# First scatter's ranking: running counts in two PSUM banks used in turn, each count product issued into both

## What is computed

```
edge_index = jnp.stack([src, dst])
x = _layernorm(x + _L0_gnn_ref(x, edge_index, edge_weight, ...))     # three hops: segment_sum(edge_weight * z[col], row)
x = _layernorm(x + _L1_gnn_ref(x, node_type_8, src, dst, edge_type_8, ...))   # typed attention
x = _layernorm(x + _L2_gnn_ref(x, edge_index, ...))                  # attention with leaky relu
x = _layernorm(x + _L3_gnn_ref(x, edge_index, ...))                  # attention, softmax by source
```

## Time and profile before

| | us |
|---|---|
| median of three runs | 10584.68 |
| lowest and highest run | 10577.77, 10587.44 |
| profiled execution, its own time | 10581.93 |
| its span in the profile | 10580.2 |
| TensorE busy | 7483.1 (71%) |
| VectorE busy | 6768.2 (64%) |
| GpSimd busy | 7062.8 (67%) |
| ScalarE busy | 2110.4 (20%) |

### The profile page before, as it was taken

How to read it: one execution, slowest core, us unless ns; L and a number is a source line. 1 busy time by engine, 2 the same in 40 slices (tenths; PEclk the granted TensorE clock), 3 DMA queues, 4 the chain that set the end, 5 groups by cost and what they waited for, 6 DMA issues and landing times. The chain is left out here.

```text
span 10580.2 us, 161564 instructions
## 1 busy us (share of the span) xinstructions
PE 7483.1 (71%) x38345; PEld 5959.2 (56%) x38346; DVE 6768.2 (64%) x21194; ACT 2110.4 (20%) x5705; POOL 7062.8 (67%) x7404
## 2 busy tenths in 40 slices
PE   6999755549998899739105666557774588857776
PEld 4666544436776677624004565456664588846665
DVE  7555566657776777637106777678886455547776
ACT  0333200001111111112002222223332222222222
POOL 1777577767777777767776777057772577737774
PEclk9999955555555555569557888789996655556665
DMA  0000122232223222235104333122222322244443
GB/s 18 2 2 2 24 53 53 52 56 52 53 53 49 62 54 54 52 70 164 50 12 103 104 103 104 28 57 53 51 52 29 83 54 53 54 81 108 108 108 81
DMA packets 434008, 634.20 MB, mean 60 GB/s; under 512 B 163990, under 2 KB 302826, under 8 KB 433034
## 3 DMA queue, kind: packets, MB, share of 16 engines
q0 software_dynamic: 263168, 497.83, 20.3%
q1 hardware_dynamic: 170378, 131.15, 4.3%
HBM read 536.19 MB, written 92.30 MB: 59 GB/s over the span
## 5 line engine op out<-in xcount | busy, mean ns | idle before, releaser
L702 POOL DMA_INDIRECT hop_rows<-hops,k_src_other x1664 | 1571.0, 944 | 553.6 <-issue 497.8
L743 PE MATMUL hop_sums<-hop_rows,hop_weighted 128*128 128x128 f32 x4992 | 1291.8, 440 | 720.6 <-DMA hop_rows<-in_x,k_src_other 449.0
L743 PEld LDWEIGHTS hop_sums<-hop_rows,hop_weighted 128*128 128x128 f32 x4992 | 1109.9, 327 | 874.3 <-DVE hop_odd L788 539.0
L1009 POOL DMA_INDIRECT l_pass_rows<-left_table,k_dst_other x832 | 803.5, 966 | 565.7 <-POOLq L2319 292.0
L1009 POOL DMA_INDIRECT l_pass_rows<-key_table,k_src_other x832 | 787.5, 946 | 509.0 <-POOLq L1616 254.7
L1441 POOL DMA_INDIRECT l_weigh_rows<-row_table,l_weigh_ring x832 | 788.7, 948 | 386.0 <-issue 210.3
L1009 POOL DMA_INDIRECT l_pass_rows<-related,k_dst_typed x832 | 810.4, 974 | 298.1 <-issue 227.0
L702 POOL DMA_INDIRECT hop_rows<-in_x,k_src_other x832 | 785.5, 944 | 303.7 <-issue 253.2
L514 POOL DMA_INDIRECT src_sorted<-src_scatter_records,src_scatter_places x784 | 751.0, 958 | 304.2 <-issue 280.6
L885 POOL DMA_INDIRECT dst_sorted<-rec,dst_places x784 | 762.1, 972 | 277.3 <-issue 238.7
L775 DVE TENSOR_SCALAR hop_weighted<-k_numbers,k_src_place,src_weight 128x128 f32<-128x128 f32 x2496 | 849.9, 402 | 56.3 <-PE hop_sums L743 32.9
(11 more groups left out here) (402 smaller groups left out, 17383.1 us busy)
## 6 DMA issues: line engine op xcount, KB each, us to landing
related<-l_tables_rows SPq DMA_DIRECT2D x50, 1024.0 KB, 4.5
hop_rows<-hops,k_src_other POOLq DMA_INDIRECT x1664, 2.5
hop_rows<-in_x,k_src_other POOLq DMA_INDIRECT x832
l_pass_rows<-related,k_dst_typed POOLq DMA_INDIRECT x832, 2.8
l_pass_rows<-left_table,k_dst_other POOLq DMA_INDIRECT x832, 2.5
l_pass_rows<-key_table,k_src_other POOLq DMA_INDIRECT x832, 2.5
l_weigh_rows<-row_table,l_weigh_ring POOLq DMA_INDIRECT x832
src_sorted<-src_scatter_records,src_scatter_places POOLq DMA_INDIRECT x784
```

The costliest lines, as they stand in the source:

```text
L702: nc.gpsimd.indirect_dma_start(rows[:, s, g, :], None, table_in, bass.IndirectOffsetOnAxis(ap=o.other[:, c:c + 1], axis=0),).then_inc(got[ ...
L743: last = nc.tensor.matmul(sums[:, b, g, :], weighted[:, s % SLOTS, g, :], rows[:, s, g, :], start=True, stop=True)
L1009: nc.gpsimd.indirect_dma_start(rows[:, s, g, :], None, table, bass.IndirectOffsetOnAxis(ap=index[:, c:c + 1], axis=0),).then_inc(got[s], 16)
```

## The change

The table is kept in two PSUM banks. Each one gets every count product, so each product is issued twice, with one column between the two: in column c TensorE issues the product of column c-1 and that of column c into bank (c+1) mod 2, which then holds the table that column c+1 needs. ScalarE copies from bank c mod 2. The wait before the two products asks for one copy less than before (`next_copied` starts at 1), and a new wait ahead of the lookup asks for the copy of column c. The table's start is put into both banks. VectorE clears the one-hots that stand for the column before the first, and waits on line 480 for one lookup more, since the slot's last column is now also read in the next group's first one.

```diff
--- before.py
+++ after.py
@@ -378,7 +378,7 @@
         earlier = sb("earlier", [P, 2, G])
         places = sb("places", [P, SLOTS, G], I32)
         records = sb("records", [P, SLOTS, G, 4])
-        next_ps = ps("next_ps", [HIS, 512])
+        next_ps = ps("next_ps", [HIS, 2, 512])
         turned = ps("turned", [HIS, 2, G, P], BF16)
         nexts = ps("nexts", [P, 2, G, P])
         keyrow = ps("keyrow", [P, 2, G, P])
@@ -418,7 +418,7 @@
 
                         act.wait_ge(next_ready, n * G + g + 1)
                         act.wait_ge(looked, n * G + g + 2 * G - 1)
-                        nc.scalar.copy(next_sb[:, g % 2, :], next_ps[:, 0:P]).then_inc(next_copied, 1)
+                        nc.scalar.copy(next_sb[:, g % 2, :], next_ps[:, g % 2, 0:P]).then_inc(next_copied, 1)
 
             turn_onehots(0, 0)
             in_rounds(act, groups // SLOTS, a_round)
@@ -431,7 +431,10 @@
                 last.then_inc(turned_ok, 1)
 
             pe.sem_inc(looked, 2 * G)
-            nc.tensor.matmul(next_ps[:, 0:P], k.ident[0:HIS, 0:HIS], first_place[:], start=True, stop=False,
+            pe.sem_inc(next_copied, 1)
+            nc.tensor.matmul(next_ps[:, 1, 0:P], k.ident[0:HIS, 0:HIS], first_place[:], start=True, stop=False,
+                             skip_group_check=True)
+            nc.tensor.matmul(next_ps[:, 0, 0:P], k.ident[0:HIS, 0:HIS], first_place[:], start=True, stop=False,
                              skip_group_check=True).then_inc(next_ready, 1)
             pe.wait_ge(onehots, 1)
             turn_onehots(0)
@@ -445,8 +448,13 @@
                     for g in range(G):
 
                         pe.wait_ge(next_copied, n * G + g + 1)
-                        nc.tensor.matmul(next_ps[:, 0:P], oh_hi[:, s, g, :], oh_lo[:, s, g, :], start=False,
+                        s0, g0 = (s, g - 1) if g > 0 else ((s + SLOTS - 1) % SLOTS, G - 1)
+                        nc.tensor.matmul(next_ps[:, 1 - g % 2, 0:P], oh_hi[:, s0, g0, :], oh_lo[:, s0, g0, :], start=False,
+                                         stop=False, skip_group_check=True)
+                        nc.tensor.matmul(next_ps[:, 1 - g % 2, 0:P], oh_hi[:, s, g, :], oh_lo[:, s, g, :], start=False,
                                          stop=False, skip_group_check=True).then_inc(next_ready, 1)
+
+                        pe.wait_ge(next_copied, n * G + g + 2)
                         nc.tensor.matmul(nexts[:, b, g, :], oh_hi_t[:, b, g, :], next_sb[:, g % 2, :], start=True,
                                          stop=True).then_inc(looked, 1)
                         if g == 0:
@@ -467,6 +475,8 @@
                 mark(nc, oh_lo[:, s, :, :], k.numbers, keys[:, 1, here]).then_inc(onehots, 1)
 
             dve.sem_inc(ranked, 2)
+            nc.vector.memset(oh_hi[:, SLOTS - 1, G - 1, :], 0.0)
+            nc.vector.memset(oh_lo[:, SLOTS - 1, G - 1, :], 0.0)
             hot(0, 0)
             hot(1, 1)
 
@@ -477,7 +487,7 @@
 
                     dve.wait_ge(ranked, n + 1)
 
-                    dve.wait_ge(looked, n * G + G)
+                    dve.wait_ge(looked, n * G + G + 1)
                     hot(n + 2, (s + 2) % SLOTS)
 
                     dve.wait_ge(rows, n + 1)
```

## The result

The changed kernel takes 10662.36 us, the median of four runs (10653.11 to 10667.76), against 10581.23 before (10577.59 to 10587.44): a ratio of 1.0075, interval 1.0058 to 1.0093. It is 81 us slower; 86 was forecast, and the time lies inside the range.

What follows compares the result with a forecast made beforehand. TensorE was taken to pace the scatter stage itself, at 5.29 us per group. Added products cost 86 us, both wait changes 0: 10581.9 + 86 = 10667.9, expected as 10670 us (+0.8%), range 10640 to 10715.

Steps and rivals of the forecast that it cites:

- The wait isn't one: Before the scatter's count products: the 131.3 us idle "until" ScalarE's copy is TensorE's own pause, so removing it gives 0.
- from an fp32 lookup: Scatter stage: the 0.22 us pause is TensorE's own turn from an fp32 lookup to another kind of matmul.
- The price of the pair: Scatter count products on TensorE: 784 added products at 0.106 us each, 83.1 us; 86 with a small extra.
- The added 3 us: Scatter columns: a product following its like is 0.24 ahead of its lookup, not 0.23; half of at most 6 us.
- The added wait costs nothing: Wait for copy c ahead of the scatter lookup: the copy is ready in time, so it costs 0.
- Its spare: Copy ahead of the scatter lookup: ready after 0.72 us, needed after 1.30, so 0.58 us to spare.
- The clock: Scatter stage: matmuls last 0.301 us, so it runs at 1.2 GHz, and more matmuls were not expected to raise that.
- the printed 1.00: Clock printed for the scatter stage in the profile before; the prediction held that it runs at 1.2 GHz whatever this says.
- GpSimd's limit: Scatter DMAs: four per group at 1.26 us take 5.03 us against a period of 5.29, the next bound.
- rivals 1 and 2: Scatter stage faster: the copy sets the pace (-45 us, chance 4%), or the clock rises (-51 us, chance 2%).
- All else just shifts: Stages after the scatter: they start later and keep their old length.

Runs made afterwards that it cites:

- the spare copies: Changed kernel with two more table copies into spare buffers ahead of each copy: period 5.71 us, ratios 0.9997 and 1.0010.
- the paired order: Changed kernel with two columns' products issued together, then their two lookups: 10547.89 us, ratio 0.9962; on a chip with late releases 1.0047.

## Why the prediction was right

- *The wait isn't one* (the step on which the case hung): held. The changed profile has the same 0.224 us pause, the two banks without the second product leave the period at 5.29, and a copy made 0.32 us late eats 0.23 us of slack first. Its name for the pause, a turn "from an fp32 lookup", was too narrow: with a bf16 lookup a pause stands on both sides of it as well.
- *The price of the pair*, 0.106 us in a stream: held. 784 x 0.106 = 83 us; the last places moved by 83.5 us. The added 3 us for a longer gap behind a product that follows its like was wrong: the gap is 0.24 and not 0.23, but the step from the first product of a stream to the second is 0.096 and not 0.106, so the two cancel (0.096 + 0.240 - 0.230 = 0.106). The sum without these 3 us is nearer to both the stage and the median of the runs, 81 us.
- *The added wait costs nothing*: held (two banks without the second product, 5.29 us). Its spare was put at 0.58 us; in the changed kernel's timeline the copy ends 0.62 us ahead of its lookup's load, 0.57 without the 0.05 for the release. With the spare copies, 0.25 us later, 0.37 are left.
- *The clock*: products last 0.301 us after as before, so nothing rose. That the printed 1.00 was no record is confirmed by the second row of the stages after: this profile prints 1.00 for the ranked hops as well, where that of before has 0.50, and TensorE's busy time there is nearly the same (785.15 against 787.84 us). This profile's first clock record stands at 4724 us.
- *GpSimd's limit* was put at 5.03 us per group; with its DMAs back to back the paired order shows 5.06, so rivals 1 and 2 could have gained 45 us and not 51.
- *All else just shifts*: nearly. In the profiled execution the changed kernel was 83.5 us behind at the stage's end, 88 when the attention pass of the third layer started its DMAs (7023 us), and 73 at the last of them (8085 us), with the same code. In the stretches where it caught up (7500 to 8012 us before, 88 us later after) the granted clock was 0.95 and 0.92 before and 0.98 in both after, so a higher clock may have given these us back; that is not shown. The other runs of the changed kernel were 8 to 15 us longer than the profiled one, so this belongs to the spread between executions.

## What to carry to other kernels

A releaser that the profile names is a candidate and not a verdict: if a pause has the same length behind every releaser and behind none, it belongs to the engine. Take the end of the release and the start of the work: here 0.05 us between them was a wait, and of 0.28 some 0.23 was slack. Where the engine paces itself, each instruction added to it costs its place in the stream, even if it is there to free the engine of a wait, and the gain lies in fewer turns between kinds of matmuls.

## What the runs showed of the hardware

- TensorE pauses about 0.13 us beyond its stream time between the count product (128x50 stationary) and the lookup (50x128), 0.24 from start to load against 0.106 in a stream, with an fp32 lookup and with a bf16 one alike. After an fp32 lookup the next load comes 0.35 us after its last pass started, 0.21 being the pass; after a bf16 one, 0.21 us, about two steps of a bf16 stream. Products and one-hot transposes of one stationary shape follow each other at 0.106 us, with a semaphore wait between them or without.
- With TensorE busy for 1037 of 1040 us, its matmuls ran at the lower clock for the whole stage (0.301 us, as at a granted clock of 0.50). The Trainium skill, TensorE: Matmul & The Clock Gate, section "What's actually happening", has activity release the throttle; no run here had a stage of this kind in which it did.
- The same program, the kernel before, took 10581 us where the change was timed, 10586 in one experiment and 13470 to 13670 in the others. In the latter, releases come late, and not in this stage alone. With two products the last places are written at 1610 us there and at 1324 in the changed kernel, some 290 us of about 3010; the DMAs of the third layer's attention pass take 1526 us from first to last, against 1062. The kernel with two products in one bank, timeline:

```profile
501.04 0.31 PE L450 MATMUL src_scatter_next_ps<-src_scatter_oh_lo,src_scatter_oh_hi 128*50 128x128 bf16 x1
...
503.61 0.26 ACT L421 COPY src_scatter_next_sb<-src_scatter_next_ps 50x128 f32<-50x128 f32 x1 [4.42 <-remote]
```

The product ended at 501.35 and the copy, 0.11 us behind it elsewhere, came 2.26 us behind it. The instructions themselves last as long as elsewhere (product 0.31 us, copy 0.26, scatter DMA 0.96). The cause stays open.
